# The bias of an attention block's last layer as a column loaded on ScalarE's queue, and new orders for all engines

## The reference

```python
# attention block, on n0 = layernorm(x)
n  = ln(n0, g, b)
W1 = gelu(n @ h1_w1 + h1_b1) @ h1_w2 + h1_b2          # 128 -> 512 -> 128
W2 = gelu(n @ h2_w1 + h2_b1) @ h2_w2 + h2_b2
t  = ln(gelu(tril(W1 @ W2.T) @ n), g, b)
a  = n0 + gelu(ln(n0 + t, g, b) @ fm_w1 + fm_b1) @ fm_w2 + fm_b2
x  = x + layernorm(a)
# feed-forward block, on y = layernorm(x); the weights are -1, 0 or 1 with a scale per output
h  = silu(y @ w1.T * s1) * (y @ w2.T * s2)            # 128 -> 512
h  = gelu(h @ h1.T * hs1)                             # 512 -> 512, "a" in the kernel
h  = gelu(h @ h2.T * hs2)                             # 512 -> 512, "b"
x  = x + layernorm(h @ w3.T * s3)                     # 512 -> 128
```

## Time and profile before

| | us |
|---|---|
| median of the runs | 365.7 |
| span of the profiled execution | 362.6 |
| time of that execution around the span | 3.1 |
| TensorE busy | 350.1 |
| VectorE busy | 319.9 |
| ScalarE busy | 305.2 |
| GpSimd busy | 147.2 |

### The profile page before, as it was taken

The page is one execution under the profiler, slowest core; times in us unless marked ns, Lnnn a source line. Parts: engine busy times, 40 slices in busy tenths (PEclk is TensorE's granted clock), DMA queues, the critical chain, the costliest instruction groups (busy, mean ns, idle before and its releaser), DMA issues.

```text
span 362.6 us, 6039 instructions
## 1 busy us (share of the span) xinstructions
PE 350.1 (97%) x1788; PEld 289.2 (80%) x1788; DVE 319.9 (88%) x954; ACT 305.2 (84%) x552; POOL 147.2 (41%) x213
## 2 busy tenths in 40 slices
PE   6989999999999999999999999999999999999993
PEld 5867687778888888888888888888888887788992
DVE  5889999999999999889989989998969998886936
ACT  5999999997779979988599888897799569959892
POOL 4168842860546052504750286003920174044411
PEclk9999999999999999999999999999999999999998
DMA  7507020000000000000010001000000001001111
GB/s 233 174 14 245 4 60 1 1 2 1 3 0 0 2 0 2 17 13 2 1 29 3 0 0 33 0 1 2 1 0 2 0 2 31 0 2 29 32 30 33
DMA packets 8804, 9.08 MB, mean 25 GB/s; under 512 B 577, under 2 KB 6722, under 8 KB 8770
## 3 DMA queue, kind: packets, MB, share of 16 engines
q1 hardware_dynamic: 8226, 8.41, 7.7%
q10 hardware_dynamic: 544, 0.26, 0.2%
HBM read 6.57 MB, written 2.10 MB: 24 GB/s over the span
## 4 chain that ended last, share of the span: by engine, by line
PE 67%; ACT 13%; DVE 10%; issue 5%; DMA 2%; POOL 1%; SPq 1%; POOLq 0%; DVEq 0%; ACTq 0%
PE bank L1224 8%; PE bank L1226 8%; PE bank L1240 6%; PE bank L1241 6%; PE bank L1123 4%; PE bank L1104 4%; PE bank L1108 4%; PE bank L1105 4%; PE bank L1120 4%; PE bank L1121 4%; PE bank L1206 4%; PE bank L1209 4%; ACT h_hidden_hi L510 3%; PE bank L1046 2%; ACT bank L515 2%
## 5 line engine op out<-in xcount | busy, mean ns | idle before, releaser
L715 DVE TENSOR_TENSOR ffn_gate_lo<-bank,ffn_gate_hi 128x512 fp32r<-128x512 f32 (+1 forms) x72 | 44.1, 626 | 6.0 <-ACT bank L584 4.9
L510 ACT ACTIVATE h_hidden_hi<-bank,cols 128x512 fp32r<-128x512 f32 x64 | 46.1, 760 | 3.5 <-PE bank L1108 3.2
L515 ACT ACTIVATE bank<-bank,cols 128x512 f32<-128x512 f32 x64 | 45.1, 739 | 0.3
L715 DVE TENSOR_TENSOR h_hidden_lo<-bank,h_hidden_hi 128x512 fp32r<-128x512 f32 x64 | 43.0, 681 | 2.5 <-ACT bank L515 2.5
L584 ACT ACTIVATE bank<-bank,cols 128x512 f32<-128x512 f32 (+1 forms) x72 | 43.7, 620 | 0.7
L1224 PE MATMUL bank<-ffn_gate_hi,ffn_w_hi 128*128 128x512 f32 (+1 forms) x108 | 40.5, 381 | 0.2 <-DVE ffn_gate_lo L715 0.2
L1226 PE MATMUL bank<-ffn_gate_lo,ffn_w_hi 128*128 128x512 f32 (+1 forms) x108 | 39.3, 370 | 0.2 <-DVE ffn_gate_lo L715 0.2
L578 ACT ACTIVATE ffn_h_hi<-bank,cols 128x512 fp32r<-128x512 f32 (+1 forms) x36 | 23.0, 646 | 13.5 <-PE bank L1226 8.3
L578 ACT ACTIVATE ffn_gate_hi<-bank,cols 128x512 fp32r<-128x512 f32 (+1 forms) x36 | 23.2, 647 | 10.6 <-PE bank L1226 8.3
L364 POOL TENSOR_TENSOR XR<-X,ln_x_r 128x512 f32<-128x512 f32 x8 | 8.3, 1042 | 53.6 <-DVE bank L861 53.4
L715 DVE TENSOR_TENSOR ffn_h_lo<-bank,ffn_h_hi 128x512 fp32r<-128x512 f32 (+1 forms) x36 | 22.0, 626 | 8.0 <-ACT bank L584 7.8
(11 more groups left out here) (164 smaller groups left out, 1132.3 us busy)
## 6 DMA issues: line engine op xcount, KB each, us to landing
raw<-ffn_w SPq DMA_DIRECT2D x5, 512.0 KB, 3.9
out<-X SPq DMA_DIRECT2D x7, 256.0 KB, 2.3
raw<-attn_w SPq DMA_DIRECT2D x6, 256.0 KB, 4.9
X<-x SPq DMA_DIRECT2D x3, 256.0 KB, 5.6
raw<-ffn_w SPq DMA_DIRECT2D x1, 256.0 KB, 3.2
X<-x ACTq DMA_DIRECT2D x1, 128.0 KB, 2.5
X<-x SPq DMA_DIRECT2D x1, 128.0 KB, 2.3
out<-X SPq DMA_DIRECT2D x1, 128.0 KB, 1.8
```

The lines of the kernel that those rows point to most:

```text
L510: nc.scalar.activation(dst, bank(f"{L}u{j}", c)[:, :], ACT.Gelu, bias=bias_of(L, j)).then_inc(*hi[L].done(c, j))
L515: nc.scalar.activation(u[:, :], u[:, :], ACT.Gelu, bias=bias_of(L, j)).then_inc(*act2[L].done(c, j))
L715: return nc.vector.tensor_tensor(dst, whole, high.bitcast(f32), ALU.subtract)
```

## The change

The row becomes a column. SyncE no longer loads it; ScalarE issues, behind its half of x chunk 0, a transfer that lays the 128 numbers one to a partition straight into the tile `fm_b2`. TensorE's product with the row and VectorE's copy are gone. `fm_evict` of chunk 0 waits for the transfer. Beside this, every engine's list of steps is written in a new order, and `TURNS` gives the banks in a new one. The steps themselves are the same on every engine.

```diff
@@ TURNS: all eight strings are new; of the first bank
-    "rb.0 fb.0 h1d.1 h1u3.2 fmd.0 h2u0.3 h2u2.3 flag.0 fmd.1 q3.0 a2.0 b0.0 mT.2 fmu2.2 p3.1 fT.0 h1u1.5 fmu2.3 q1.2 "
+    "rb.0 h1u0.0 h1u3.0 h2u1.1 h1d.2 h1u2.3 h2u2.3 flag.0 fmu2.1 nT.4 p3.0 q3.0 a2.0 h1u2.4 mT.2 fmu1.2 fmu3.2 a0.1 "
...
-        b2_row = M[0:1, 0, :]
...
-            sp.dma_start(b2_row, rows[2:3, :]).then_inc(b2_in, 16)
...
             act.dma_start(X[:, 2:4, :], xv[:, 2:4, :]).then_inc(x_in_half, 16)
+            act.dma_start(fm_b2[:, :], rows[2:3, :].rearrange("o d -> d o")).then_inc(b2_in, 16)
...
                 if c:
                     act.wait_ge(*oT.at(c - 1))
+                else:
+                    act.wait_ge(b2_in, 16)
                 act.wait_ge(*down["fm"].at(c, J - 1))
...
                 dve.wait_ge(*fm_b.at(0))
-                nc.vector.tensor_scalar(fm_b2[:, :], bank("fb", 0)[:, J:J + 1], 1.0, None, ALU.mult)
...
-                    nc.tensor.matmul(bank("fb", 0)[:, j:j + 1], raw[:, w:w + P], cols[:, C_B:C_B + 1], start=True, stop=True)
-                pe.wait_ge(b2_in, 16)
-                last = nc.tensor.matmul(bank("fb", 0)[:, J:J + 1], b2_row, ones[0:1, :], start=True, stop=True)
+                    last = nc.tensor.matmul(bank("fb", 0)[:, j:j + 1], raw[:, w:w + P], cols[:, C_B:C_B + 1], start=True, stop=True)
                 last.then_inc(*fm_b.done(0))
```

More of the change, by code:

```diff
@@ L1186, in _ @@
+            down_mm("fm", 0, 1)
             pe.wait_ge(*lo_flagged.at(0))
@@ new lines, in stream @@
+                gate_mm("q", 2, 0); down_mm("fm", 3, 1); gate_mm("p", 3, 0); up_mm("h1", 0, 4); scores(0, 3)
+                product("a", 1, 0, 0); scores(1, 3); product("a", 1, 1, 0); o_transpose(1); gate_mm("q", 3, 0)
+                up_mm("h1", 1, 4); product("a", 0, 0, 0); product("a", 0, 1, 0); product("a", 1, 2, 0)
+                product("a", 0, 2, 0); product("a", 0, 3, 0); product("a", 1, 3, 0); layer_mm("a", 2, 0); t_product(3)
+                layer_mm("a", 3, 0); product("b", 1, 0, 0); product("b", 0, 0, 0); product("b", 0, 1, 0)
@@ new lines, in stream @@
+                product("a", 0, 0, 2); t_transpose(4); product("a", 0, 1, 2); o_transpose(3); up_mm("h2", 2, 5)
+                product("a", 0, 2, 2); product("a", 0, 3, 2); down_mm("h1", 1, 5); product("a", 1, 0, 2)
+                product("a", 1, 1, 2); down_mm("h1", 2, 5); product("a", 1, 2, 2); product("a", 1, 3, 2)
+                layer_mm("a", 2, 2); layer_mm("a", 3, 2); down_mm("h2", 0, 5); product("b", 0, 0, 2); down_mm("h1", 3, 5)
+                product("b", 1, 0, 2); product("b", 1, 1, 2); product("b", 0, 1, 2); up_mm("h2", 3, 5)
@@ new lines, in stream @@
+                down_mm("fm", 0, 4); up_mm("fm", 3, 4); down_mm("fm", 1, 4); scores(0, 5); gate_mm("p", 3, 3)
+                gate_mm("q", 1, 3); scores(1, 5); up_mm("h1", 1, 6); down_mm("fm", 2, 4); product("a", 1, 0, 3)
+                product("a", 0, 0, 3); down_mm("fm", 3, 4); gate_mm("q", 2, 3); gate_mm("q", 3, 3); product("a", 0, 1, 3)
+                o_transpose(4); up_mm("h2", 0, 6); up_mm("h1", 2, 6); product("a", 1, 1, 3); product("a", 1, 2, 3)
+                t_product(5); f_transpose(2); product("a", 0, 2, 3); up_mm("h2", 1, 6); t_transpose(5)
@@ new lines, in stream @@
+                product("a", 0, 3, 3); product("a", 1, 3, 3); layer_mm("a", 2, 3); layer_mm("a", 3, 3)
+                product("b", 0, 0, 3); down_mm("h1", 0, 6); product("b", 0, 1, 3); down_mm("h1", 1, 6)
+                down_mm("h1", 2, 6); up_mm("h1", 3, 6); up_mm("h2", 2, 6); product("b", 0, 2, 3); product("b", 1, 0, 3)
+                product("b", 1, 1, 3); product("b", 0, 3, 3); product("b", 1, 2, 3); up_mm("h2", 3, 6)
+                product("b", 1, 3, 3); layer_mm("b", 2, 3); y_transpose(4); n_transpose(7); down_mm("h1", 3, 6)
@@ new lines, in stream @@
+                layer_mm("b", 3, 3); m_transpose(5); gate_mm("p", 0, 4); gate_mm("q", 0, 4); up_mm("h1", 0, 7)
+                gate_mm("p", 1, 4); product("w3", 0, 0, 3); product("w3", 0, 1, 3); up_mm("fm", 0, 5)
+                product("w3", 0, 2, 3); up_mm("fm", 1, 5); gate_mm("p", 2, 4); down_mm("h2", 0, 6); product("w3", 0, 3, 3)
+                gate_mm("q", 1, 4); down_mm("h2", 1, 6); down_mm("h2", 2, 6); down_mm("h2", 3, 6); up_mm("fm", 2, 5)
+                up_mm("fm", 3, 5); gate_mm("p", 3, 4); down_mm("fm", 0, 5); gate_mm("q", 2, 4); up_mm("h1", 1, 7)
@@ new lines, in stream @@
+                product("a", 1, 0, 5); product("a", 0, 2, 5); product("a", 1, 1, 5); product("a", 1, 2, 5)
+                product("a", 0, 3, 5); product("a", 1, 3, 5); layer_mm("a", 2, 5); layer_mm("a", 3, 5)
+                product("b", 1, 0, 5); product("b", 0, 0, 5); product("b", 0, 1, 5); product("b", 0, 2, 5)
+                product("b", 1, 1, 5); product("b", 1, 2, 5); product("b", 0, 3, 5); product("b", 1, 3, 5)
+                layer_mm("b", 2, 5); y_transpose(6); layer_mm("b", 3, 5); product("w3", 0, 0, 5); m_transpose(7)
@@ new lines, in stream @@
+                product("a", 1, 1, 6); product("a", 0, 3, 6); product("a", 1, 2, 6); product("a", 1, 3, 6)
+                layer_mm("a", 2, 6); layer_mm("a", 3, 6); product("b", 0, 0, 6); product("b", 0, 1, 6)
+                product("b", 1, 0, 6); product("b", 1, 1, 6); product("b", 1, 2, 6); product("b", 0, 2, 6)
+                product("b", 0, 3, 6); product("b", 1, 3, 6); y_transpose(7); layer_mm("b", 2, 6); gate_mm("p", 0, 7)
+                gate_mm("p", 0, 8); gate_mm("p", 1, 7); layer_mm("b", 3, 6); gate_mm("q", 0, 7); gate_mm("p", 1, 8)
@@ new lines, in stream @@
+                layer_mm("a", 2, 7); gate_mm("q", 2, 8); layer_mm("a", 3, 7); gate_mm("q", 3, 8); product("a", 0, 1, 8)
+                product("a", 1, 0, 8); product("a", 1, 1, 8); product("b", 1, 0, 7); product("a", 0, 2, 8)
+                product("a", 1, 2, 8); product("b", 0, 0, 7); product("b", 1, 1, 7); product("b", 0, 1, 7)
+                product("a", 0, 3, 8); product("b", 0, 2, 7); product("a", 1, 3, 8); layer_mm("a", 2, 8)
+                product("b", 0, 3, 7); layer_mm("a", 3, 8); product("b", 1, 2, 7); product("b", 1, 3, 7)
@@ new lines, in stream @@
+                layer_mm("b", 2, 7); product("b", 0, 0, 8); layer_mm("b", 3, 7); product("b", 0, 1, 8)
+                product("b", 0, 2, 8); product("b", 0, 3, 8); product("b", 1, 0, 8); product("b", 1, 1, 8)
+                product("b", 1, 2, 8); product("b", 1, 3, 8); layer_mm("b", 2, 8); layer_mm("b", 3, 8)
+                product("w3", 0, 0, 7); product("w3", 0, 1, 7); product("w3", 0, 2, 7); product("w3", 0, 3, 7)
+                product("w3", 0, 0, 8); product("w3", 0, 1, 8); product("w3", 0, 2, 8); product("w3", 0, 3, 8)
```

532 lines of the change are left out of this document (252 added, 280 removed), and 43 rows, old and new, of the table TURNS.

## The result

The changed kernel takes 372.1 us (median of 4 runs, 372.01 to 372.26) against 365.8 for the kernel before on the same chip (365.67 to 366.59). The ratio is 1.017 with an interval of 1.0155 to 1.0184. The forecast was 364.5 and its range ended at 366.7.

A forecast was written before the change was run, and what follows sets the result against it. ScalarE, VectorE close behind, bounds the first 80 us, then TensorE. From 365.7: start -0.8, 80 to 300 us +0.3, attention end -0.8, tail +0.2 make -1.1, with 0.1 for the bias product: 364.5 us, range 362.3 to 366.7.

The forecast's parts named there:

- 80 to 300 us: Middle stretch, TensorE never waiting: new orders can only add, one or two waits, +0.3 us.
- the first 80 us: Up to chunk 0's first gate product: same steps per engine, only reordered, so the product comes 0.8 us earlier.
- The prediction's own signs of being wrong: Weight pieces 3 and 4 landing late, TensorE idle over 0.5 us in 80-300 us, ScalarE over 0.3 before 80.
- The start, -0.8: ScalarE's first GELU: without the bias row weights land 0.9 us sooner, less 0.1 for the column.
- The column's price, 0.1: The column's 128 pieces of 4 bytes in the DMA engines delay what follows by 0.1 us; 2.3 kept as rival.
- The late attention waits: End of the attention part: chunk 7's mT and oT transpose waits nearly go, -1.0 us; together with gate wait -0.8.
- the gate wait near 336 us: Late attention part: 20 matmuls in place of 21 before the product reading chunk 7's gate, wait grows 0.2 us.
- The tail, +0.2: Last steps: w3's evict behind the last GELU gives -0.38 us, centring between statistics and aggregate +0.60, net +0.2.
- The fourth, new waits between 80 and 300 us: Rival: two or three TensorE waits of 0.5 to 0.8 us there, +1.5 us, 365.7 us; chance 0.10.
- An early order that leaves ScalarE idle: Case for slower: the new early order leaves ScalarE idle; chance 0.05.
- Slower by the column: Rival: the column's small pieces delay every later weight piece by 2.3 us, 366.7 us; chance 0.08, half slower.
- The base: Starting time for the sum: span 362.6 us plus 3.1 us around it, 365.7 us, also the median shown.

The follow-up runs named there:

- a_pool: Changed kernel with GpSimd's order mended: steps moved so 128x512 operations miss VectorE's norm, three waits left; 367.3 us, ratio 1.0068 to the kernel before.
- b_col: Kernel before with only the bias as a column on ScalarE's queue, old orders and bank turns kept; 364.6 us, ratio 0.9987.
- b_col2: Kernel before with the bias column and two steps moved later: ScalarE's split of weight piece 5 and VectorE's low half of it; 365.1 us, ratio 0.9996.
- a_pool2: Changed kernel with GpSimd's order mended and the last steps laid as in the kernel before; 367.4 us on another chip, ratio 1.0049.
- b_read: Kernel before with four useless 128x256 SBUF-reading operations added on GpSimd beside VectorE's norm of chunk 2; ratio 1.0025.
- a_hold1: Changed kernel with one wait added: GpSimd holds its 128x512 work until VectorE's norm of chunk 2 is done; 370.5 us, ratio 1.0153.
- a_row: Changed kernel with the bias as a row again (SyncE's queue, TensorE product, VectorE copy), new orders and turns kept; 371.7 us, ratio 1.0184.

## Why the prediction was wrong

*What failed* is the step "80 to 300 us. TensorE waits for nothing there, so new orders can only add. VectorE is busy 202.56 and ScalarE 181.73 of 220 us, so both have room", priced at 0.3 us, and the same reasoning for the first 80 us ("ScalarE has the same work ahead of that product"), priced at -0.8. Both counted steps and busy time. The steps were the same, as forecast. Their durations were not, because a duration depends on what GpSimd does beside it, and I never laid GpSimd's list next to VectorE's, though its order changed too. Most of the loss, 4.9 of 6.0 us at the last sum, came from it.

The prediction's own signs of being wrong came: TensorE idle for 2.84 us between 80 and 300 us (its limit was 0.5) and ScalarE for 2.03 us in 20 to 40 us alone (its limit was 0.3). How the loss builds up is seen at chunk 7's y transpose, read by ScalarE near the end of the attention part, before, in the changed kernel and in `a_pool`:

```profile
328.38 0.59 ACT L552 ACTIVATE yT_hi<-bank 128x512 fp32r<-128x512 f32 x1
```

```profile
334.10 0.60 ACT L552 ACTIVATE yT_hi<-bank 128x512 fp32r<-128x512 f32 x1
```

```profile
329.18 0.60 ACT L552 ACTIVATE yT_hi<-bank 128x512 fp32r<-128x512 f32 x1
```

The changed kernel is 5.7 us late there. With the 1.7 us of the first gate product (next), some 4.0 us arose between the two places, where the prediction had +0.3, and the last 0.3 us behind them.

The first gate product, which was to come 0.8 us sooner, shows the early part. Before, in the changed kernel, and in `a_pool`:

```profile
81.22 0.39 PE L1206 MATMUL bank<-yT_hi,ffn_w_hi 128*128 128x512 f32 x1
```

```profile
82.96 0.39 PE L1215 MATMUL bank<-yT_hi,ffn_w_hi 128*128 128x512 f32 x1
```

```profile
81.33 0.39 PE L1215 MATMUL bank<-yT_hi,ffn_w_hi 128*128 128x512 f32 x1
```

It came 1.7 us later, 1.6 of which the mended GpSimd order takes back. So 0.8 us of gain was 0.1 us of loss even without the overlaps from 30 us on.

*The start, -0.8.* The first GELU did come 0.8 us earlier in the changed kernel:

```profile
10.38 1.25 ACT L508 ACTIVATE h_hidden_hi<-bank,cols 128x512 fp32r<-128x512 f32 x2
```

against 11.17. The number was right by luck and the reason wrong: the first GELU varies by more than a microsecond between executions, with the row and without it (above). It was also worth far less than I put in. In `b_col` the first GELU stands at 11.55 us and in `b_col2`, which has two steps moved as well, at 10.21, and their first gate products at 81.66 and 81.21: of 1.3 us at the start about 0.45 arrives.

*The column's price, 0.1, and its rival at 2.3.* Right about the size: `b_col` costs nothing that can be measured, though the column is many packets where the row was one of 512 bytes (ScalarE's queue has 688 packets in place of 544, SyncE's 8224 in place of 8226). It landed 2.9 us after its issue in the changed kernel and 2.6 us in `b_col`.

*The late attention waits.* The waits on OTA and M that the earlier trace rows shows near the end of the attention part are gone. The changed kernel's list from 300 us on names only this:

```profile
PE bank L1080 <- ACT raw L590: 0.4, 1, 0.4
```

That wait was there before too, with 0.6 us. So the step held for the two transposes. It was wrong on the gate wait near 336 us, which was to grow by 0.2 us and is gone as well. The 0.8 us was not isolated by a run.

*The tail, +0.2.* VectorE's last steps in the changed kernel:

```profile
363.34 0.50 DVE L928 BATCH_NORM_STATS2 ln_f_st<-bank 128x6 f32<-128x128 f32 x2
363.75 0.59 DVE L943 TENSOR_SCALAR raw<-bank,ln_f_mv 128x128 f32<-128x128 f32 x2
364.26 0.24 DVE L934 BATCH_NORM_AGGREGATE ln_f_mv<-ln_f_st 128x2 f32<-128x6 f32 x2
...
365.13 1.13 DVE L952 SCALAR_TENSOR_TENSOR X<-raw,ln_f_r,X 128x128 f32<-128x128 f32 x4
```

The centring stands where it was expected, at the length it had the earlier trace rows, but it puts the aggregate off by 0.39 us and not by 0.60: the aggregate starts 0.92 us behind the start of its statistics, 0.53 us before. From the last product of w3 to the last sum it is 3.33 us in the changed kernel and 2.96 before. That is not a loss of the whole: with the old tail put back (`a_pool2`) the 2.96 us come back, but the last product itself starts 0.65 us later than in `a_pool`, and no time came back.

*The rivals.* The fourth, new waits between 80 and 300 us, had the right place, at 365.7 us with a chance of 0.10; the four waits found there sum to 2.8 us where it had 1.5, and it had nothing for the first 80 us. An early order that leaves ScalarE idle had a chance of 0.05 and no mechanism; it is what the first 80 us look like. No rival had a mechanism by which the same steps take longer. "Slower by the column" was tested by `b_col` and fell.

*The base.* The prediction added 3.1 us around the span to 362.6; as said above, that joins two executions. Its sum is a difference to the median and is not touched by it.

*What stays open.* With the overlaps from 30 us on away, 1.1 us (last sum) to 2.5 us (the ratio 1.0068) are left. They lie in no single wait: `a_pool` is behind the kernel before by 0.1 us at the first gate product, by 0.8 at chunk 7's y transpose and by 1.1 at the last sum. One overlap that stretches an operation is left in it that no run took away: at 12.8 us VectorE's low half of a weight piece takes 1.40 us in place of 0.69, beside GpSimd's `n_tok_lo` of 128x512 (13.1 us in the changed kernel); the kernel before has a smaller one, 0.94 us, at 24.4. Which of the orders on ScalarE, VectorE or TensorE costs the rest was not tried.

## What to carry to other kernels

When a change reorders several engines, lay the lists of VectorE and GpSimd side by side, not only each against its old self: a VectorE operation with two SBUF operands that TensorE will soon wait for should not stand beside a large GpSimd operation that reads SBUF. How much it costs depends on the slack behind it: 1.6 us of stretching in `b_read` can't be told from none. Look at the largest duration of a group, not its mean; one group of four took 3.09 us where its like take 1.1, while its line's median stayed at 0.34. Where such a pair can't be moved, a wait on the engine that has time can make the kernel faster.

## What the runs showed of the hardware

- GpSimd's pow on 128x4 elements is shown 1.0 to 1.34 us long. One of 1.25 us, at 34.66 us in the kernel before, holds VectorE by nothing (1.10 us for four operations beside it). A 128x512 tensor_tensor of 1.3 us holds one of VectorE's operations to its own end, and four of 128x256 hold four, which take 0.64 to 0.77 us each in place of 0.35. The Trainium skill (SBUF — State Buffer, SBUF: two separate sides) says the pair is held for the whole instruction; for the small pow no such hold shows.
- A VectorE operation that reads one of its operands from PSUM is not stretched: `ffn_gate_lo` at 110.39 us takes 0.69 us with `y_centre` of GpSimd beside it from 110.73 on, its length elsewhere.
- A stall that TensorE suffers early is partly free: of 2.5 us that `a_hold1` had won at 41 us against the changed kernel, 1.0 us was left at 49 us; against `a_row`, whose clock stayed up, it was 1.3 and 0.5 us.
